# A decoder layer on one core: context values times output weights made once in a first phase, and cross-attention exps taken from PSUM with the negated maximum as bias

## What is computed

```python
x = layernorm(x + self_attention(x))                  # 16 heads of 16, causal
q = (x @ w_q)   ; k = ctx @ w_k ; v = ctx @ w_v        # 16 heads of 64, ctx has 77 rows
attn = softmax(q k^T / 8)                              # per head, 256 x 77
x = layernorm(x + (attn @ v, heads side by side) @ w_o)
x = layernorm(x + ffn(x))                              # 256 -> 1024 -> 1024 -> 256, relu, +-1 weights
```

## Time and profile before

| what | us |
|---|---|
| median of 3 runs | 2335.62 (2334.43 to 2338.11) |
| the profiled execution | 2333.06 |
| its span on the core, first to last instruction | 2331.3 |
| TensorE busy | 2233.6 (96%) |
| VectorE busy | 1485.0 (64%) |
| ScalarE busy | 970.2 (42%) |
| GpSimd busy | 482.0 (21%) |
| mean granted TensorE clock | 0.987 |

### The profile page before, as it was taken

How to read it: one execution, slowest core, us unless ns; L and a number is a source line. 1 busy time by engine, 2 the same in 40 slices (tenths; PEclk the granted TensorE clock), 3 DMA queues, 4 the chain that set the end, 5 groups by cost and what they waited for, 6 DMA issues and landing times.

```text
span 2331.3 us, 52778 instructions
## 1 busy us (share of the span) xinstructions
PE 2233.6 (96%) x18516; PEld 1847.7 (79%) x18516; DVE 1485.0 (64%) x4685; ACT 970.2 (42%) x1797; POOL 482.0 (21%) x751
## 2 busy tenths in 40 slices
PE   7967899999999999999999999999999999999997
PEld 6856787888888888788888888888888888888876
DVE  3435666667667666667676666676676666676763
ACT  3313444444444444444444444444444444444432
POOL 2001212222222122212222222222221222122220
PEclk9978999999999999999999999999999999999999
DMA  6753332132333331233333322323333212233300
GB/s 209 228 115 53 54 58 45 39 50 37 56 56 56 56 50 41 42 44 49 56 56 56 56 42 39 47 41 56 56 56 56 48 40 44 40 53 56 56 25 10
DMA packets 150504, 135.85 MB, mean 58 GB/s; under 512 B 47746, under 2 KB 141986, under 8 KB 150402
## 3 DMA queue, kind: packets, MB, share of 16 engines
q1 hardware_dynamic: 150468, 135.37, 31.3%
HBM read 39.10 MB, written 28.59 MB: 29 GB/s over the span
## 4 chain that ended last, share of the span: by engine, by line
PE 81%; DVE 10%; issue 4%; ACT 3%; DMA 2%; POOL 1%; SPq 0%; DVEq 0%; POOLq 0%
PE ps L1028 10%; PE ps L1029 9%; PE ps L1169 9%; PE ps L988 8%; PE ps L1155 6%; PE ps L1011 5%; PE ps L1141 4%; PE ps L1082 4%; PE ps L1069 4%; PE ps L997 4%; DVE max L736 3%; PE ps L1039 3%; PE ps L1040 2%; PE ps L970 2%; PE ps L977 2%
## 5 line engine op out<-in xcount | busy, mean ns | idle before, releaser
L1028 PE MATMUL ps<-r_h,w 128*128 128x256 f16 x2048 | 464.4, 274 | 1.9 <-DVE r_l L682 1.9
L1029 PE MATMUL ps<-r_l,w 128*128 128x256 f16 x2048 | 462.1, 273 | 0.0
L471 ACT ACTIVATE r_h<-ps 128x512 f16<-128x512 f32 x256 | 152.6, 596 | 524.1 <-PE ps L1029 516.4
L697 DVE CUSTOM_DVE_ANT_0 junk<-ps,causal 128x128 bf16<-128x128 f32 (+1 forms) x1024 | 316.2, 353 | 60.1 <-PE ps L1058 53.8
L419 POOL TENSOR_TENSOR p<-p,inv 128x308 f32<-128x308 f32 x256 | 179.0, 699 | 479.5 <-DVE inv L753 479.5
L682 DVE SCALAR_TENSOR_TENSOR r_l<-ps,r_h 128x512 f16<-128x512 f32 x256 | 176.1, 688 | 119.5 <-ACT r_h L471 119.5
L524 ACT ACTIVATE probs<-ps 128x768 f32<-128x768 f32 x256 | 206.9, 809 | 106.9 <-PE ps L1069 106.8
L412 POOL TENSOR_SCALAR_AFFINE_SELECT probs<-probs 128x512 f32<-128x512 f32 x256 | 163.3, 638 | 393.8 <-ACT probs L524 393.7
L1028 PEld LDWEIGHTS ps<-r_h,w 128*128 128x128 f16 x2048 | 200.1, 98 | 49.6 <-issue 23.5
L1029 PEld LDWEIGHTS ps<-r_l,w 128*128 128x128 f16 x2048 | 200.9, 98 | 20.7
L758 DVE TENSOR_TENSOR o_l<-ps,o_h 128x512 fp32r<-128x512 f32 x128 | 88.5, 691 | 191.0 <-ACT o_h L516 190.6
(11 more groups left out here) (140 smaller groups left out, 4729.3 us busy)
## 6 DMA issues: line engine op xcount, KB each, us to landing
q_st<-o_h SPq DMA_DIRECT2D x192, 128.0 KB
k_bd<-o_h SPq DMA_DIRECT2D x192, 128.0 KB, 6.7
q<-q SPq DMA_DIRECT2D x128, 128.0 KB, 2.1
v_scratch<-v_out SPq DMA_DIRECT2D x44, 224.0 KB, 2.3
k_bd<-k_scratch SPq DMA_DIRECT2D x64, 154.0 KB
v<-v_scratch SPq DMA_DIRECT2D x32, 308.0 KB
x_in<-in_x SPq DMA_DIRECT2D x32, 256.0 KB, 4.6
out<-y SPq DMA_DIRECT2D x32, 256.0 KB, 2.2
```

The lines of the kernel that those rows point to most:

```text
L697: dve.tensor_tensor_reduce(out=junk[:, e, b * P:b * P + width], in0=ps[:, bank + b, e * width:(e + 1) * width], in1=causal[:, (1 - b) * P: ...
L1028: pe.matmul(dst, w1[:, kk, m * P:(m + 1) * P], r0_h[:, kk, :], start=kk == 0, stop=False)
L1029: last = pe.matmul(dst, w1[:, kk, m * P:(m + 1) * P], r0_l[:, kk, :], start=False, stop=kk == KF - 1)
```

## The change

1. **Values times output weights.** The first phase makes values transposed (`context_values`), splits them, and multiplies the 64 rows of each head with that head's 64 rows of `w_o` (`value_outputs`): for a context row and a head a row of 256, kept in scratch as `vo_d` (2 x 2464 x 2048 in f32) in place of `v2_d` (2464 x 1024). `w_o` and its split leave SBUF after that. A block loads its 1232 rows of 256 (`load_value_outputs`), ScalarE makes their high part (`value_outputs_high`) and GpSimd their low part.
2. **Cross part.** Probabilities lie as [token, half, context row, head of the half], so the 616 of a half are contiguous and are transposed in five tiles (four of 128, one of 104). ScalarE and VectorE split each (`cross_probs`, `cross_probs_low`), and `cross_output` multiplies with `vo`, six matmuls a tile, into banks 6 and 7. `cross_values`, `cross_projection` and the split between them are gone.
3. **Exps.** VectorE takes the minimum of the negated scores (`cross_low`; the query weights carry the minus), `cross_below` is gone, and ScalarE makes four exps a unit from PSUM, with the minimum as bias and scale -1. The bank is free only after them (`a_e2`).
4. **Order.** Scores by query go to bank 2 (6 for n = 3 and 5), n = 3 waits for the residual of the block, n = 7 and two of the maxima move into the next block, and ten of the sixteen parts of `layer1` move into the cross part. In the first phase keys and values have one bank each, and the weights come in two parts.

```diff
-            def cross_below(i, t):
-                dve.wait_ge(d_m2, nth(i, KX, t + 1))
-                dve.tensor_tensor(p2[:, t], ps[:, 4 + t % 2, 0:4 * SK].rearrange("p (j k) -> p j k", j=4),
-                                  max2[:, t, :].unsqueeze(2).to_broadcast([P, 4, SK]), ALU.subtract).then_inc(d_b2, 1)
...
             def cross_exp(i, t):
-                act.wait_ge(d_b2, nth(i, KX, t + 1))
-                act.activation(p2[:, t], p2[:, t], ACT.Exp).then_inc(a_e2, 1)
...
+                act.wait_ge(d_m2, nth(i, KX, t + 1))
+                heads = unit_probs(t)
+                for j in range(4):
+                    last = act.activation(heads[:, j // 2, j % 2, :], ps[:, 4 + t % 2, j * SK:(j + 1) * SK], ACT.Exp,
+                                          bias=low2[:, t, j:j + 1], scale=-1.0)
+                last.then_inc(a_e2, 1)
...
+            def value_outputs(g, m):
...
+                for c, read in enumerate((a_vp, d_vp)):
+                    if k >= 1:
+                        pe.wait_ge(read, k)
+                    for a in range(2 * c, min(2 * c + 2, GROUPS[g])):
+                        for n, (v2t, w) in enumerate(((v2t_h, wo_h), (v2t_h, wo_l), (v2t_l, wo_h))):
+                            for e in range(2):
+                                half = slice(64 * e, 64 * e + 64)
+                                last = pe.matmul(ps[0:CT, 4 + 2 * c + e, (a % 2) * D:(a % 2 + 1) * D],
+                                                 v2t[k % 2][half, a * CT:(a + 1) * CT], w[half, m, :],
+                                                 start=n == 0, stop=n == 2)
...
+            def cross_output(i, g, c):
...
+                for n in P2T_UNITS[c]:
+                    rows, at = tile_rows(n), tile_at(g, n)
+                    for k, (p, w) in enumerate(((p2t_h, vo_h), (p2t_h, vo_l), (p2t_l, vo_h))):
+                        for b in range(TB):
+                            last = pe.matmul(ps[:, 6 + b, 0:D], p[0:rows, at, b * P:(b + 1) * P], w[0:rows, at, :],
...
+                if n == 3 and after_cross:
+                    pe.wait_ge(d_y2, nth(i, 1, 0))
...
                 scores_by_key(i, 0)
-                transposed_max(i, 1)
+                if f is not None:
+                    pe.wait_ge(d_mx, nth(i, 2 * H, 24))
                 scores_by_key(i, 1)
                 filler2(0)
+                if f is not None:
+                    scores_by_query(i, 7)
                 scores_by_key(i, 2)
                 filler2(1)
                 scores_by_key(i, 3)
+                transposed_max(i, 1)
+                filler2(2)
...
+                if more:
+                    scores_by_query(i + 1, 1)
                 cross_scores(i, 5)
-                cross_transposes(i, 1)
+                layer1_until(f, 16, 18)
                 cross_scores(i, 6)
...
+                layer1_until(f, 18, 20)
                 cross_scores(i, 7)
...
+                cross_transposes(i, 0, 0, more)
+                cross_transposes(i, 0, 1)
+                layer1_until(f, 20, 22)
+                cross_output(i, 0, 0)
+                cross_transposes(i, 0, 2)
+                cross_output(i, 0, 1)
+                cross_output(i, 0, 2)
+                layer1_until(f, 22, 24)
+                cross_transposes(i, 1, 0)
+                cross_transposes(i, 1, 1)
+                layer1_until(f, 24, 26)
+                cross_output(i, 1, 0)
+                cross_transposes(i, 1, 2)
+                cross_output(i, 1, 1)
+                cross_output(i, 1, 2)
                 if more:
                     scores_by_query(i + 1, 2)
...
+                layer1_until(f, 26, 27)
                 if more:
                     scores_by_query(i + 1, 3)
...
+                layer1_until(f, 27, 28)
                 if more:
                     scores_by_query(i + 1, 4)
...
+                layer1_until(f, 28, 29)
                 if more:
                     scores_by_query(i + 1, 5)
...
+                layer1_until(f, 29, 30)
                 if more:
                     transposed_max(i + 1, 0)
...
+                layer1_until(f, 30, 32)
                 if more:
                     scores_by_query(i + 1, 6)
...
```

VectorE's order in and after the cross part, and ScalarE's (the diff cut to the calls):

```diff
             def attention(i, first, f, g, more=True):
+                if not first:
+                    self_max(i, 6)
+                    self_max(i, 7)
...
+                    if t == 4 and more:
+                        self_max(i + 1, 1)
+                    if t == KX - 2:
+                        cross_probs_low(i, 0, 0)
                 cross_inverse(i, KX - 2)
+                cross_probs_low(i, 0, 1)
                 cross_sum(i, KX - 1)
-                cross_output_low(i, 0)
                 cross_inverse(i, KX - 1)
...
+                cross_probs_low(i, 0, 2)
+                for c in range(3):
+                    cross_probs_low(i, 1, c)
                 if more:
                     self_max(i + 1, 2)
...
                 cross_exp(i, 4)
-                cross_probs(i, 0)
                 cross_exp(i, 5)
-                cross_probs(i, 1)
+                cross_probs(i, 0, 0)
                 cross_exp(i, 6)
-                cross_probs(i, 2)
+                cross_probs(i, 0, 1)
+                cross_probs(i, 0, 2)
                 cross_exp(i, 7)
```

575 lines of the change are left out of this document (321 added, 254 removed).

## The result

The changed kernel takes **2830.3 us** (median of four runs, 2828.1 to 2831.3), the kernel before beside it 2335.0 (2333.9 to 2338.1): **1.212 times as long**, 95% interval 1.210 to 1.214. The forecast was 2513 and its range ended at 2610. The direction was right, the size was not: the change costs 495 us, and 178 were forecast.

What follows compares the result with a forecast made beforehand. TensorE, with 81% of the chain of waits, was taken to bound the kernel. 2333.06 us profiled, plus 78 for the first phase and 102 for 30 blocks, gave 2513 us; the 8-in-10 range was 2345 to 2610.

Steps and rivals of the forecast that it cites:

- the walk: Hand-followed order of a block from its first cross query matmul: cross part ends at 28.5 us, layer0 starts at 49.5.
- First phase, +78 forecast: Before the blocks: TensorE ends near 214 us where it ended near 139, +75, and +3 for a larger last save.
- Switches and the first matmul of a unit: First phase: entering and leaving the tiled form costs TensorE 0.25 us for each of 48 units, 12 us (0 to 15).
- Stalls behind VectorE's weight jobs: First phase: with one bank for values, VectorE's long jobs stall TensorE, 7 us (0 to 12).
- The low end, +56: Lower end for the first phase: 12 us less with full overlap of the halves and 7 less without stalls.
- A block without the hold, +3.5 forecast: Each block takes 3.5 us longer, about 69.6: 5.2 + 0.9 less work and waits, 9.6 of new waits.
- Scores 3 on the residual: Behind the cross part, TensorE's scores 3 wait 2.1 us for VectorE's residual add, the largest new wait.
- TensorE's work: In a block: 14.7 us of transposes, `cross_values` and projection gone, 9.5 of transposes and `cross_output` added, 5.2 less.
- The strided copies: Basis for the exps' stores: 128 elements took 430 ns strided, about 312 unstrided, so up to 0.08 us more each.
- Serial halves and strided exps: Rival: first phase +126 us, blocks +5.0 each, 2609 us in total; chance 0.14.
- The faster rival: TensorE stays the bound of a block and its work alone counts, 5.2 to 6.1 us less: 2246 us; chance 0.15.
- the distance of cross queries: Sign: cross queries of two successive blocks lie near 69.6 us apart; under 64 the prediction is wrong.

## Why the prediction was right or wrong

- **The step that failed**: "On GpSimd and ScalarE the splits of `vo` (2560 columns) fall where both have long gaps: hidden." ScalarE's three were hidden: no wait in the view names them. GpSimd's were in its gap, and cost at least 218 us all the same (235 by the run without them). The step asked whether GpSimd is free and what waits for its result. It didn't ask what else GpSimd's work keeps from running. The rows for that were at hand. In the trace before, VectorE's normalization starts in the very place where GpSimd's gap begins, and TensorE's transposes of x1 follow at 1201.27:

```profile
1199.73 0.71 POOL L431 TENSOR_TENSOR rstd<-var_eps,minus_half 128x2 f32<-128x2 f32 x1
...
1200.47 0.73 DVE L676 TENSOR_SCALAR x<-x,mv,rstd 128x256 f32<-128x256 f32 x2
```

- **What is left.** Of the 317 us between forecast and result, the run with the splits behind the normalization leaves 99: some 80 of them are blocks that are 2.6 us longer than forecast, see below, the rest small terms.
- **The clock**: the forecast had it at 1.00 throughout. The longest wait of the walk was 2.1 us; the one not foreseen was 5.18, and 54 us of the 218 are the clock's.
- **First phase, +78 forecast, +80.5 measured.** Right in sum, less so in its terms. The matmuls of `value_outputs` are 0.059 each, not 0.070: 62 us, the lower end. Switches and the first matmul of a unit took about 0.2 (24 matmuls in 1.60 us from 100.38 to 101.98, of which 1.42 at the even rate), 9 us for 48 units where 12 were taken. Stalls behind VectorE's weight jobs were 9.4 us, not 7. TensorE ended at 216.3, not 214, with a stretch at the lower level of the clock (0.50 from 55.4 to 60 us) behind a stall of 4.2. The text's "near 215" for the load of the first input was short of its own sum, by which it is 220; it started near 222 and ended at 225.0. The low end, +56, is 19 off the +75; off the +78 it is +59. The Trainium skill (TensorE: Matmul & The Clock Gate, Part 3) had been quoted for full overlap of the halves; the trace agrees, with pairs 0.118 apart.
- **A block without the hold, +3.5 forecast, +5.7 measured** (71.87 against 66.14 in the windows, 6.1 in the mean over all blocks, of which the hold at its later place is 0.5). The waits were right: 9.54 us of idleness in that block, and 9.6 of new waits forecast. Scores 3 on the residual 1.83 (2.1), `cross_output(0, 2)` 1.09 (1.2), exps together 2.04 (2.0), scores 5 and 6 0.54 and 0.34 (0.5 each). The mis-sized term is **TensorE's work**: 3.0 us less (65.36 to 62.33), not 5.2. Part of it is seen: the 60 `cross_output` matmuls take about 7.5 us, not 7.1, and four score matmuls behind a wait take 0.79 in place of 0.68; if each of some 14 waits costs 0.1 on top (an estimate), that makes 1.8 of 2.2. The rest is open.
- **Walk**: the cross part ended at 29.7 (28.5 forecast), layer0 started at 51.9 (49.5). The order of events was as walked.
- **Exps**: contiguous 0.97 a unit, with the kernel's stride 1.04 to 1.06; 0.98 was taken and 1.3 was the upper end. The strided copies gave the right price for one exp (up to 0.08, measured 0.07); that each of the four would add it was wrong, since the starts stay 0.21 apart. And yet the stride costs 22 us, also through VectorE's sum and GpSimd's product (0.90, before 0.70), which the forecast left at their old length.
- **The rivals.** "Serial halves and strided exps" came nearest in time, for wrong reasons: no half was serial. The faster rival was 584 us off. None had a mechanism with GpSimd in it, so the range couldn't hold the result.
- **What would show it**: the distance of cross queries was to be near 69.6. It was 78.9, and with the splits behind, 72.2. So by that sign alone, with the hold taken away, the walk was 2.6 us short.

## What to carry to other kernels

Before work is put into a gap of GpSimd, ask which VectorE operations run in that stretch: here copies and tensor_scalar from SBUF, and tensor_tensor and scalar_tensor_tensor of two SBUF operands, waited for GpSimd's whole job. A new order can also make two old instructions meet, as the normalization of x2 and `xb` did here. Put the job behind the critical one, or cut it into pieces no longer than the delay that the path can bear. The wait of TensorE of 5.18 us cost more than its length, since the work behind it ran at the lower clock (54 us of 218).

## What the runs showed of the hardware that was not expected

- A GpSimd job of 2.34 us holds a VectorE tensor_scalar, copy or tensor_tensor of SBUF operands for its whole length; with a PSUM operand, and for tensor_reduce, reciprocal and bn_stats, the difference is at most 0.01 us. In the changed kernel the second of the pair was held over two queued jobs (6.0 us for the pair with three jobs, 1.53 with ten).
- Useless matmuls in an idle time of 5.18 us made a kernel 54 us faster.
- Matmuls of the two row halves ran in twos at 0.118 a pair, also when the program had three of one half before three of the other.
- A stride of 32 B costs ScalarE's exp of 77 elements, which stores with it, 70 ns alone and nothing between starts, VectorE's sum of 308 elements 255 ns, and GpSimd's product 200 ns.
- 24 loads a block in place of four, with no more bytes, cost 6 us a block, by the wait for a small DMA that SyncE issues behind them.
